# Adjacency tiles loaded and scanned piece by piece, with two pieces in flight, in a sparse graph-attention kernel

## The reference

```python
h = jnp.maximum(_layernorm(x, axis=-1), 0.0)
hh = (h @ W.T).reshape(n, H, D)
s_src = jnp.einsum('nhd,hd->nh', hh, a_src)
s_dst = jnp.einsum('nhd,hd->nh', hh, a_dst)
attn = s_src[:, None, :] + s_dst[None, :, :] + adj[:, :, None] * We[:, 0] + be
attn = jnp.where((adj > 0)[:, :, None], attn, -jnp.inf)
attn = jax.nn.softmax(jax.nn.leaky_relu(attn, 0.2), axis=1)
out = x + jnp.einsum('ijh,jhd->ihd', attn, hh).reshape(n, H * D) + h @ Wr.T + br
```

## Time and profile before

| | |
|---|---|
| median of 3 runs | 2688.48 us (2686.38 to 2694.1) |
| profiled execution | 2684.95 us, of which the span in the trace is 2683.3 us |
| DVE | 2132.3 us busy, 79% of the span |
| POOL | 1485.7 us busy, 55% |
| ACT, PE | 1246.5 us (46%), 1235.0 us (46%) |
| DMA | 512.79 MB, mean 191 GB/s; SP's queue 319.60 MB, POOL's queue 191.61 MB |

### The profile page before, as it was taken

One profiled execution on the slowest core, in us unless ns is written; L12 is line 12 of the kernel. 1 busy time (PEld: TensorE's weight loads), 2 busy tenths in 40 slices (PEclk: granted clock), 3 DMA queues, 4 the chain that ended last, 5 costly groups with the idle time before them and its releaser, 6 DMA issues.

```text
span 2683.3 us, 27007 instructions
## 1 busy us (share of the span) xinstructions
PE 1235.0 (46%) x5305; PEld 934.2 (35%) x5306; DVE 2132.3 (79%) x4852; ACT 1246.5 (46%) x4898; POOL 1485.7 (55%) x1666
## 2 busy tenths in 40 slices
PE   6990022503334367446424524533341453518885
PEld 4660022402324245334322512422241342416664
DVE  3448959998998898999889988988997841259992
ACT  2320030221245498667546546444542655826662
POOL 5772656756675777777777476277347437710000
PEclk9995556757666676666666666666665666759998
DMA  3665656686676877877777677678668614477660
GB/s 114 195 228 191 216 131 195 167 249 178 179 226 192 225 240 225 245 229 243 229 224 239 199 233 222 183 231 233 208 193 234 200 39 100 95 225 173 157 156 3
DMA packets 226527, 512.79 MB, mean 191 GB/s; under 512 B 98280, under 2 KB 116400, under 8 KB 224208
## 3 DMA queue, kind: packets, MB, share of 16 engines
q1 hardware_dynamic: 151280, 319.60, 37.2%
q0 software_dynamic: 74960, 191.61, 28.1%
q10 hardware_dynamic: 144, 0.13, 0.0%
HBM read 475.19 MB, written 36.03 MB: 191 GB/s over the span
## 4 chain that ended last, share of the span: by engine, by line
DMA 56%; issue 18%; PE 10%; DVE 6%; POOL 6%; ACT 2%; SPq 1%; POOLq 0%; DVEq 0%; ACTq 0%; PEldq 0%
DMA adj_sb<-in_adj_dram 40%; DMA arena<-table,arena 8%; DMA arena<-table,own 6%; POOL arena L493 5%; PE banks L1058 2%; PE banks L1052 2%; ACT arena L947 1%; PE banks L1101 1%; DVE work L619 1%; PE banks L1079 1%; DVE work L615 1%; PE banks L1055 1%; PE banks L1154 1%; PE banks L1144 1%; DMA out_dram<-w_all,arena 1%
## 5 line engine op out<-in xcount | busy, mean ns | idle before, releaser
L493 POOL DMA_INDIRECT arena<-table,arena x943 | 972.6, 1031 | 354.5 <-issue 231.2
L1079 PE MATMUL banks<-arena,ident 128*128 128x256 f32 x1268 | 426.9, 513 | 1142.1 <-DVE arena L755 1142.1
L947 ACT ACTIVATE arena<-arena,prob 128x32 f32<-128x32 f32 x4024 | 859.5, 306 | 2.1
L1079 PEld LDWEIGHTS banks<-arena,ident 128*128 128x128 f32 x1268 | 332.6, 268 | 1234.8 <-issue 984.6
L615 DVE MAX8 work<-adj_sb 128x8 f32<-128x184 f32 (+51 forms) x624 | 580.9, 1005 | 116.0 <-DMA adj_sb<-in_adj_dram 115.5
L619 DVE FIND_INDEX8 work<-work,adj_sb 128x8 uint32<-128x184 f32 (+51 forms) x624 | 618.6, 1013 | 0.0
L942 ACT ACTIVATE prob<-pre 128x104 f32<-128x104 f32 (+26 forms) x63 | 20.3, 322 | 965.6 <-DVE pre L739 965.6
L1085 PE MATMUL banks<-arena,ident 128*128 128x256 f32 x1006 | 312.6, 442 | 106.3 <-ACT arena L947 106.2
L493 POOL DMA_INDIRECT arena<-table,own x194 | 202.2, 1042 | 157.4 <-DMA arena<-table,own 55.6
L1085 PEld LDWEIGHTS banks<-arena,ident 128*128 128x128 f32 x1006 | 197.3, 212 | 209.0 <-ACT arena L947 188.5
L932 ACT ACTIVATE pre<-arena,we_all 128x13 f32<-128x13 f32 (+23 forms) x480 | 146.5, 400 | 80.1 <-DMA arena<-lists 80.1
(11 more groups left out here) (140 smaller groups left out, 1789.2 us busy)
## 6 DMA issues: line engine op xcount, KB each, us to landing
adj_sb<-in_adj_dram SPq DMA_DIRECT2D x504, 512.0 KB, 4.0
arena<-dst_rows SPq DMA_DIRECT2D x16, 2048.0 KB, 8.5
arena<-table,arena POOLq DMA_INDIRECT x943, 3.5
table<-arena POOLq DMA_DIRECT2D x32, 264.0 KB, 2.9
arena<-in_x_dram SPq DMA_DIRECT2D x32, 256.0 KB, 3.0
resid<-arena POOLq DMA_DIRECT2D x32, 256.0 KB, 2.6
out_dram<-arena POOLq DMA_DIRECT2D x32, 256.0 KB, 2.8
work<-table SPq DMA_DIRECT2D x8, 1024.0 KB, 10.9
```

Of the source, the lines that this page charges most:

```text
L493: pool.indirect_dma_start(gath[:, un.slot(k), :], None, table[:, :], bass.IndirectOffsetOnAxis(ap=rec[:, k, 0:1], axis=0), bounds_check=N ...
L947: last = s.activation(g, g, ACT.Copy, scale=prob[:, b, k * H + h:k * H + h + 1])
L1079: last = m.matmul(ps_sum[:, u % 2, :], ident[:, :], gath[:, un.slot(k), 0:HD], start=(k == 0), stop=False)
```

## The change

Loading: every piece, whatever the tile, now has one of two semaphores (*lanes*), even pieces on one and odd pieces on the other, for each of the two buffers. From piece 2 on, SP waits for the landing of the piece two before, so two are in flight. Between tiles no landing is waited for. Instead of waiting for the whole scan of find c - 2, piece n waits only for those `max_index` instructions that read columns up to the end of piece n.

Scanning: `max` of segment s waits for the pieces that the segment needs. `max_index` of segment s - 1 stands behind `max` of segment s. Each `max` increments `maxed` and each `max_index` increments `scanned` by one, and each `max_index` waits for its own `max`. The number of `max` and `max_index` instructions and their operands are unchanged.

```diff
+        segs_before = [sum(so.segs for so in sources[:c]) for c in range(len(sources))]
+        def scans_of(so, n):
+            return sum(lo < (n + 1) * PIECE for lo in segments(so.segs, so.power)[:-1])
...
-                if c >= 2:
-                    sp.wait_ge(S["scanned"], c - 1)
                 for n in range(PIECES):
                     cols = slice(n * PIECE, (n + 1) * PIECE)
-                    if n and so.t >= 16:
-                        sp.wait_ge(S[f"adj_in{b}"], 16 * (c // 2 * PIECES + n))
-                    sp.dma_start(adj_sb[:, b, cols], load_adj(so.t)[:, cols]).then_inc(S[f"adj_in{b}"], 16)
+                    lane = S[f"adj_in{b}{n % 2}"]
+                    if c >= 2:
+                        sp.wait_ge(S["scanned"], segs_before[c - 2] + scans_of(sources[c - 2], n))
+                    if n >= 2:
+                        sp.wait_ge(lane, 16 * (c // 2 * (PIECES // 2) + n // 2))
+                    sp.dma_start(adj_sb[:, b, cols], load_adj(so.t)[:, cols]).then_inc(lane, 16)
...
-                dve.wait_ge(S[f"adj_in{b}"], (c // 2 + 1) * 16 * PIECES)
                 a = adj_sb[:, b, :]
+                def index(s):
+                    dve.wait_ge(S["maxed"], segs_before[c] + s + 1)
+                    v.max_index(idx8[:, 8 * s:8 * s + 8], val8[:, 8 * s:8 * s + 8],
+                                a[:, bounds[s]:bounds[s + 1]]).then_inc(S["scanned"], 1)
                 for s in range(so.segs):
-                    last = v.max(val8[:, 8 * s:8 * s + 8], a[:, bounds[s]:bounds[s + 1]])
-                last.then_inc(S["maxed"], 1)
-                dve.wait_ge(S["maxed"], c + 1)
-                for s in range(so.segs):
-                    last = v.max_index(idx8[:, 8 * s:8 * s + 8], val8[:, 8 * s:8 * s + 8],
-                                       a[:, bounds[s]:bounds[s + 1]])
-                last.then_inc(S["scanned"], 1)
+                    pieces = -(-bounds[s + 1] // PIECE)
+                    for lane in range(2):
+                        if pieces > lane:
+                            dve.wait_ge(S[f"adj_in{b}{lane}"], 16 * (c // 2 * (PIECES // 2) + (pieces - lane + 1) // 2))
+                    v.max(val8[:, 8 * s:8 * s + 8], a[:, bounds[s]:bounds[s + 1]]).then_inc(S["maxed"], 1)
+                    if s:
+                        index(s - 1)
+                index(so.segs - 1)
                 v.tensor_reduce(flag8[:, :], val8[:, 0:VN].rearrange("p (s e) -> p s e", e=8)[:, :, 7],
                                 AX_X, ALU.max).then_inc(S["flag_a"], 1)
-                dve.wait_ge(S["scanned"], c + 1)
+                dve.wait_ge(S["scanned"], segs_before[c] + so.segs)
```

More of the change, by code:

```diff
@@ L303, in gat_kernel @@
             "lower_set", "consts_set",
-            "adj_in0", "adj_in1", "maxed", "scanned", "jshift", "masked_keys", "keyed", "sorted_",
+            "adj_in00", "adj_in01", "adj_in10", "adj_in11", "maxed", "scanned", "jshift", "masked_keys", "keyed", "sorted_",
             "dec", "decoded", "pre_done", "flag_a", "flag_b",
```

## The result

The changed kernel takes 2584.78 us (median; 2584.57 to 2589.83), the kernel before 2687.43 us beside it (2681.77 to 2694.1). The ratio is 0.9622, with a 95% interval of 0.9596 to 0.9647: faster. The forecast was 2578 us, 6.8 us less. The profiled executions took 2684.95 and 2584.57 us, with spans of 2683.3 and 2582.7 us; all that follows is about these 100.6 us of span.

The account below looks back on a forecast made before the run. DVE, the busiest engine, was taken to be held by gathers up to unit 23 and by adjacency waits behind it. 23 + 16 - 17 + 88.9 = 111 us off 2684.95 gives 2574, plus 3.5 for the median: 2578 us; range 2545 to 2640.

Parts of the forecast that it names:

- Stretch 3: Unit 23 (1391.5 us) to the end of the last find: adjacency waits of DVE go, gaining 88.9 us.
- The hand-offs inside the scan: New semaphore updates and waits of `max` and `max_index` on DVE: taken as 0; exposed, 0.12 us each.
- Stretch 2: Unit 3's softmax to unit 23: gathers limit; 16 us gained from waits, 17 us lost to slower gathers.
- Stretch 1: 209 us to unit 3's softmax (676 us): two pieces in flight where eight were, faster gathers, 23 us gained.
- the pitch of 1.44: POOL's time per gather in us with two pieces in flight, 0.05 above one piece's 1.39; assumed for both early stretches.
- the first rival: Gathers become the bound from 836 us on, pitch 1.61, each 0.22 us slower: 2654 us, chance 0.16.
- Two pieces cost the gathers as much as eight: Gathers bound DVE up to unit 28, nothing gained early; net gain 34 us, 2654 us, chance 0.16.
- Gathers not slowed: Rival: time per gather 1.39 us or less, 132 to 152 us gained, 2556 to 2536 us; below 2550, chance 0.08.
- Exposed hand-offs: Rival: each of 1,248 scan instructions on DVE pays 0.12 us, 150 us more work, 2727 us; chance 0.06.
- Nothing happens: Rival: a pair of adjacency pieces takes twice as long as one, nothing gained, 2688 us; chance 0.05.
- The tail: From the last `max_index` to the end, last gathers and dense tile: claimed untouched, 519 us as before.

Follow-up runs that it names:

- f1: Kernel before with two adjacency pieces in flight, but whole-tile hand-over and the old scan order: 2604.37 us, ratio 0.9682.
- f2: Changed kernel with one adjacency piece in flight instead of two, hand-over in pieces kept: 2647.99 us, ratio 0.9836.
- g3: Changed kernel with up to eight adjacency pieces in flight, a lane for each and no wait for a landing: 2614.23 us, ratio 0.9731.
- g1: Changed kernel with one adjacency piece in flight for finds 0 to 35 and two from find 36 on: 2555.28 us, ratio 0.9523.
- g2: Changed kernel with eight gather lanes instead of four: 2537.22 us, ratio 0.9446.
- both edits: Changed kernel with one piece in flight to find 35, then two, plus eight gather lanes; two disturbed chips: 3056.88 us (1.059) and 2994.16 us (1.0456).

## Why the prediction was right, and where it was not

**Stretch 3: right.** Forecast 88.9 us, measured 91.0. The rows forecast: adjacency waits near 0 (0.4 us), finds 25.4 us apart (25.26). The 2 us above the forecast lie within the 4 us of the next point. f1 shows that the second lane does this, f2 that the pieces do not. The rival that two pieces take twice as long as one fails on the landing: the median piece lands in 4.5 us with two in flight, and in 3.9 us with one (f2). From the first issue of a find to its last landing it is 23.7 us in the mean of finds 36 to 61; I had taken "some 20", and 25.4 was allowed.

**The hand-offs inside the scan: free, and a little better.** I took 0. Two consecutive steps of the scan in find 36:

```profile
1386.02 0.91 DVE L632 MAX8 work<-adj_sb 128x8 f32<-128x167 f32 x2
1386.85 0.07 DVE L624 MATCH_VALUE_LOAD work<-work,adj_sb 128x8 f32 x1
1386.91 0.33 DVE L624 FIND_INDEX8 work<-work,adj_sb 128x8 uint32<-128x167 f32 x1
1387.15 1.01 DVE L632 MAX8 work<-adj_sb 128x8 f32<-128x836 f32 x1
1388.08 0.07 DVE L624 MATCH_VALUE_LOAD work<-work,adj_sb 128x8 f32 x1
```

The `max` that follows a `max_index` starts 0.09 us before that one's modelled end, and the value load behind a `max` 0.08 us before, as in the earlier trace rows. In find 36 of the kernel before, the value load behind the last `max` starts at 1411.84 us, 0.03 us after the end at 1402.75 + 9.06:

```profile
1402.75 9.06 DVE L615 MAX8 work<-adj_sb 128x8 f32<-128x167 f32 x7 [4.14 <-DMA adj_sb<-in_adj_dram]
1411.84 0.09 DVE L619 MATCH_VALUE_LOAD work<-work,adj_sb 128x8 f32 x1
```

The old order had one exposed wait a find, between its last `max` and its first `max_index`, and the new one hides it. A seven-segment find lasts 18.47 us in place of 18.62; in f1, which keeps the old order, it is 18.61. So 0.15 us a find, or some 9 us over 63 finds, is a gain that the prediction did not have. It was put at nothing though the earlier trace rows held its size, 0.12 us. The 27 finds of stretch 3 carry 4 us of it.

**Stretch 2: the pitch right, its start not.** I forecast that the gathers up to unit 23 would take 17 us longer. From POOL's start on unit 7 to the issue of unit 23's last gather it took 549.1 us where it had taken 532.7: 16.4 us, or 0.048 a gather against the 0.05 that I chose. Counted as the prediction counted, by busy time and two waits, the pitch is (352.23 + 88.9 + 40.2) / 339 = 1.42 us, 0.03 above the 1.39 of before; with the waits for stores it is 1.44. So 1.44 is met by the one count and not by the other. The issue itself:

```profile
1370.89 1.00 POOL L500 DMA_INDIRECT arena<-table,arena  x1 [0.30 <-issue]
```

In the earlier trace rows this was 1368.62 us; now it takes 8.1 us from here until unit 23's softmax starts, 1370.9 + 8.1 = 1379.0. The forecast's own working gives 1368.6 - 23 + 17 + 7.0 = 1369.6. The 9.4 us between are 8.9 of a start that came 14.1 us earlier and not 23, 1.1 of the landing, less 0.6 of the pitch. Which unit binds was also incomplete: I had looked at unit 23 alone, while units 15 and 16 bind before it, and at unit 16 only 2.8 of unit 3's 17.1 us are left. It did not matter for the sum, as the adjacency waits of the earlier trace rows come behind it and went.

**Stretch 1: the term that was mis-sized.** Forecast 23 us, measured 17.1, of which 2.3 had come before the first scan and some 1.6 us (12 finds) is the hidden wait. So the loads gave about 13. The step that failed is the pitch of 1.44 carried over from the long window: units 1 to 3 stand at 1.60 to 1.72, above the 1.5 that the prediction had named as its own sign of being wrong. DVE's wait ahead of unit 3 is 11.9 us where it said near 0. From the start of a unit's first gather to the end of its last, divided by the count:

| pieces in flight | unit 0 | unit 1 | unit 2 | unit 3 |
|---|---|---|---|---|
| eight, whole-tile hand-over (before) | 1.52 | 1.80 | 1.61 | 1.58 |
| two, whole-tile hand-over (f1) | 1.49 | 1.75 | 1.63 | 1.59 |
| up to eight, in pieces (g3) | 1.43 | 1.75 | 1.65 | 1.62 |
| two, in pieces (after) | 1.41 | 1.72 | 1.62 | 1.60 |
| one, in pieces (f2) | 1.41 | 1.72 | 1.57 | 1.57 |
| one, in pieces (g1, the same program up to here) | 1.40 | 1.67 | 1.53 | 1.52 |
| two, in pieces, eight gather lanes (g2) | 1.30 | 1.64 | 1.62 | 1.39 |

I had read the 1.61 of the earlier trace rows as the price of eight pieces in flight, 0.22 above one. The table denies most of it. f2 and g1 are one program on two chips and differ by 0.05, so hundredths can't be read from it. But from eight (before) to two (after) units 2 and 3 do not come down at all, and with one in flight they are at 1.52 to 1.57, 0.01 to 0.08 below before. Between g1 and g3, on one chip, lie 0.12 and 0.10. Unit 3 comes down with more gather lanes as well (1.39), unit 2 does not (1.62), so what sets the rest of their pitch is not settled. What did shrink with the change is unit 0, by 0.11, most of it (0.08) through the hand-over in pieces, which I had not counted at all. This misreading is also behind the price of the first rival: in the long window g3 stands (575 - 550) / 339 = 0.07 us a gather above two, where the rival had 0.22 above one, though g3 has 2.3 pieces in flight there and not eight.

**The rivals.** *Two pieces cost the gathers as much as eight:* not in the long window. The pitch there is 1.42 to 1.44 and not 1.61, and the windows of 538, 550 and 575 us for one, two and up to eight, and unit 23 at 1359.8, 1379.0 and 1411.6 us, tell them apart. At units 2 and 3, though, two cost what eight had cost. By the round-robin rule in the Trainium skill, DMA: Bandwidth & Descriptors, section Queues, rings and completion order, two and eight would cost the same once the adjacency ring never runs dry; by the windows of g3 and the changed kernel the ring's depth counts also beyond two, or the ring does run dry with two. The trace does not tell which. *Gathers not slowed:* no, by 16.4 us. *Exposed hand-offs:* no, by the scan above. *Nothing happens:* no, by f1.

**The tail.** It was held at 519 us; it is 521.5 against 518.6, 2.9 us longer. The other kernels on undisturbed chips have 515.8 to 520.0, so this moves by itself from kernel to kernel, and I have no cause for it.

The whole: 17.1 forecast as 23, then -4.6 (17.1 to 12.5 at unit 23) forecast as -1, then 91.0 forecast as 88.9, then -2.9 forecast as 0: 100.6 in place of 111. That is 10.4 us short. The median is only 6.8 us off by luck: the forecast added 3.5 us from the profiled execution to the median, and after the change the two lie 0.2 us apart. Without the scan's hidden waits, a gain that the prediction had put at nothing, the shortfall would have been larger.

## What to carry to other kernels

When one stream of transfers feeds the busiest engine and another shares the DMA engines with it, give the first just as many transfers in flight as its deadline asks, stage by stage. On the undisturbed chips one in flight was best while gathers set the pace and two once the scan did, and that split (2555 us) beat two throughout (2585) and up to eight throughout (2614). Two lanes were worth more when each piece was handed over by the consumer's own steps than in bursts behind a whole tile (20 us here, some 5 of which the scan's order may have given). And the price of a contended resource, read in one stage, must be checked in a second stage at the same depth before it is carried to a third: most of unit 2's 1.61 us had another cause than the one I gave it.

## What was not expected of the hardware

**Some chips hold up the vector engine beside the gathers.** On three of the five chips of the experiments the kernel before takes 2866 to 2889 us, on the other two 2686 and 2689. In every profile from the three, DVE stands idle in front of instructions whose inputs were written. (The kernel before was not profiled there.) Lines from the eight-lane kernel on the first such chip, DVE's timeline:

```profile
1005.07 0.22 DVE L666 MATCH_REPLACE8 work<-work 128x72 f32<-128x72 f32 x1
1005.20 0.35 DVE L753 TENSOR_TENSOR pre<-pre,rmax 128x192 f32<-128x192 f32 x1
1009.74 0.24 DVE L662 MAX8 work<-work 128x8 f32<-128x72 f32 x1 [4.18 <-remote]
1009.89 0.22 DVE L663 MAX8 work<-work 128x8 f32<-128x72 f32 x1
1013.93 0.09 DVE L665 MATCH_VALUE_LOAD work<-work 128x8 f32 x1 [3.83 <-issue]
```

L665 waits for L663, which ended at 1010.1 us by the same trace, and yet it starts 3.8 us later. In the changed kernel on an undisturbed chip L663 ends at 2062.46 us and L665 starts at 2062.53, with a softmax step between them. Idle times of this kind (0.25 us or longer, put down to "issue" or "remote") sum, in the sparse stage, to 105 us with the depth alone, 107 with up to eight pieces, 275 with one piece, 368 and 435 with both edits, 398 with eight gather lanes on the kernel before and 403 with them on the changed one. On the undisturbed chips they are 0 to 14 us, all of them ahead of a unit's first softmax step. There are none before the gathers begin. In the dense tile they are 1.4 to 1.8 us on either kind of chip (10 in one run). All kernels with eight gather lanes have more of them than those with four, but among those with four they range from 105 to 275, so the lanes are not all of it.

"Remote" means that the trace has a semaphore's update just before the start, but no instruction that ends near it. L662 above waits for L666, which ended at 1005.29 us, and the update that it waits for is recorded at 1009.72. On the three chips DVE has 26 to 110 such waits in each kernel's sparse stage, with updates recorded 2.3 to 3.2 us (medians) behind the end of DVE's own instruction. On the undisturbed chips it has none. So these updates do come late. What holds them up stays open; that the gathers do is argued only from where the idle times stand. ACT has the same two kinds of wait on the three chips (for instance `ACT prob L956 <- remote: 92.1, 5, 29.5` in this kernel) and neither on the others, so DVE is not alone. Why some chips do it and others not stays open too. No chip ran at two times, so chip and time are not told apart. For the choice of a kernel it decides a lot, since kernels with eight gather lanes gave 0.9446 on one chip and 1.046 to 1.062 on three others. One in flight then two, with four lanes, is what the undisturbed chips favour; it was not run with four lanes on a disturbed one.

**A piece costs little more to land with company.** The 512 KB pieces between 1400 and 2000 us, transfers and median landing, of the kernel with one, two and up to eight in flight:

```profile
adj_sb<-in_adj_dram SPq DMA_DIRECT2D x165, 512.0 KB, 3.9
```

```profile
adj_sb<-in_adj_dram SPq DMA_DIRECT2D x190, 512.0 KB, 4.5
```

```profile
adj_sb<-in_adj_dram SPq DMA_DIRECT2D x184, 512.0 KB, 4.9
```
